# An S4 layer and an int4 SwiGLU on one core: the down weights and the resolvents at another pace, and the second up sum on VectorE

## The reference, cut to what matters

```python
# attn: S4. One kernel K of 1024 taps for all rows, a causal convolution along a row
g = 2.0 / step * ((1.0 - Omega) / (1.0 + Omega))
denom = g[:, None] - Lambda[None, :]                 # 1024 roots x 64 states
cauchy = lambda v: (v[None, :] / denom).sum(-1)      # four of them
at_roots = c * (k00 - k01 * (1.0 / (1.0 + k11)) * k10)
K = ifft(at_roots, L).real
attn = irfft(rfft(u, n=2*L) * rfft(K, n=2*L))[..., :L] + D[0] * u
# ffn: SwiGLU, weights of 4 bits with a scale and a zero for every 64 inputs
Wg, Wu, Wd = dequantize(...)                         # (w - zero) * scale; inter = 2752
h = silu(xn @ Wg.T) * (xn @ Wu.T)
ffn = h @ Wd.T
```

## Time and profile before

| what | us |
|---|---|
| median of three executions | 1499.83 |
| the profiled execution's own time | 1495.27 |
| its span | 1493.5 |
| TensorE busy in the span | 1333.8 (89%) |
| VectorE busy | 957.6 (64%) |
| GpSimd busy | 674.7 (45%) |
| ScalarE busy | 457.3 (31%) |

### The profile page before, as it was taken

The page is one execution under the profiler, slowest core; times in us unless marked ns, Lnnn a source line. Parts: engine busy times, 40 slices in busy tenths (PEclk is TensorE's granted clock), DMA queues, the critical chain, the costliest instruction groups (busy, mean ns, idle before and its releaser), DMA issues. The chain is left out here.

```text
span 1493.5 us, 17048 instructions
## 1 busy us (share of the span) xinstructions
PE 1333.8 (89%) x6299; PEld 630.9 (42%) x6299; DVE 957.6 (64%) x1057; ACT 457.3 (31%) x801; POOL 674.7 (45%) x484
## 2 busy tenths in 40 slices
PE   1557899988998999989999999449999999999998
PEld 1423444433443444434444444124444444444444
DVE  4744478899999898678898988535233332432341
ACT  3533444434444354444444543221000000000000
POOL 3642466766678688687978786341000000000000
PEclk9978999999999999999999999769999999999999
DMA  5301554343433344344444443779756236335431
GB/s 177 86 29 70 225 166 131 125 133 115 132 124 117 131 134 140 124 139 134 142 134 141 139 137 112 233 247 365 248 185 222 92 109 221 92 110 196 126 101 57
DMA packets 164646, 218.09 MB, mean 146 GB/s; under 512 B 41426, under 2 KB 121940, under 8 KB 162644
## 3 DMA queue, kind: packets, MB, share of 16 engines
q1 hardware_dynamic: 163988, 209.86, 42.8%
q10 hardware_dynamic: 576, 7.14, 1.4%
HBM read 139.64 MB, written 77.34 MB: 145 GB/s over the span
## 5 line engine op out<-in xcount | busy, mean ns | idle before, releaser
L1310 PE MATMUL px<-xo,wo 128*128 128x512 f16 x2016 | 473.9, 389 | 59.1 <-ACT py L960 30.2
L1310 PEld LDWEIGHTS px<-xo,wo 128*128 128x128 f16 x2016 | 200.1, 100 | 308.7 <-issue 26.5
L684 POOL TENSOR_TENSOR wo<-wf,wo 128x512 f16<-128x512 f32 x147 | 236.5, 1619 | 71.9 <-ACT wo L918 71.9
L703 POOL TENSOR_TENSOR hs<-hf,hs 128x512 f16<-128x512 f32 x154 | 210.8, 1375 | 103.2 <-ACT hs L953 96.1
L1394 PE MATMUL px<-wd,hr 128*128 128x512 f16 x1056 | 235.0, 382 | 10.7 <-DMA wd<-w_d 10.7
L1310 PE MATMUL pz<-xo,wo 128*128 128x512 f16 x1008 | 233.6, 382 | 0.0
L1394 PEld LDWEIGHTS px<-wd,hr 128*128 128x128 f16 x1056 | 102.6, 98 | 131.1 <-DMA wd<-w_d 11.2
L1310 PEld LDWEIGHTS pz<-xo,wo 128*128 128x128 f16 x1008 | 99.5, 99 | 120.8 <-issue 4.6
L1925 DVE SCALAR_TENSOR_TENSOR acc<-px,acc 128x512 f32<-128x512 f32 x32 | 22.1, 691 | 155.3 <-PE px L1394 151.3
L953 ACT ACTIVATE hs<-hf 128x512 f16<-128x512 f32 x154 | 94.5, 621 | 80.8 <-DVE hf L1569 48.2
L693 POOL TENSOR_TENSOR ds<-wf,ds 128x512 f16<-128x512 f32 x69 | 104.2, 1511 | 33.1 <-ACT ds_more L939 20.1
(11 more groups left out here) (211 smaller groups left out, 1406.5 us busy)
## 6 DMA issues: line engine op xcount, KB each, us to landing
h_d<-hs SPq DMA_DIRECT2D x154, 256.0 KB, 3.7
hr<-h_d SPq DMA_DIRECT2D x56, 704.0 KB, 4.2
w_d<-ds SPq DMA_DIRECT2D x69, 256.0 KB, 3.9
wd<-w_d SPq DMA_DIRECT2D x4, 2816.0 KB, 12.5
sz<-in_sz_gate SPq DMA_DIRECT2D x21, 512.0 KB
sz<-in_sz_up SPq DMA_DIRECT2D x21, 512.0 KB
sz<-in_sz_down SPq DMA_DIRECT2D x20, 512.0 KB
xc_d<-xo SPq DMA_DIRECT2D x8, 1024.0 KB, 10.5
```

What stands on the lines that cost most here:

```text
L684: pool.tensor_tensor(w_dest(t, j, 1), w_place_of(j), w_dest(t, j, 0), ALU.subtract).then_inc(wlo_done, 1)
L703: pool.tensor_tensor(hs[:, j, :, 1, :], h_place_of(p, j), hs[:, j, :, 0, :], ALU.subtract)\
L1310: done = pe.matmul(bank[:, :], wo[t % 2][:, j, wp, k * P:(k + 1) * P], xo[p][:, j, xp, k, :], start=(j in (0, 3) and k == 0 and wp == 0 an ...
```

## The change

- **An even pace for the down weights.** Time is cut in half units: `split_step(n, i)` is 2(n - 3) + i. In step t each engine does its part of split t (`down_step`, on SyncE, GpSimd, ScalarE and VectorE), and words are dequantised in the steps with t mod 7 = 5 and 0. Group 0 starts in unit 2, so seven splits go by in three and a half units, and the last split is that of unit 41's first half. The order of slabs is now a list made to match, and three `ds` buffers serve all.
- **Loads of `wd`.** Each is one load of the whole `wd[j]`. `wd[0]` now lies where the weight words were and is loaded by SyncE after the last split's store; `wd[1]` and `wd[2]` by ScalarE's queue after unit 41, `wd[3]` and `wd[4]` in and after unit 43, `wd[5]` and `wd[6]` by SyncE.
- **The second up sum.** `snap_u3` and GpSimd's `c22` are gone. A `c22` on VectorE adds the bank px to `s5` into `u3`, and product 6 waits for it.
- **VectorE's order.** `c22(n)` stands ahead of `up` and of `c12(n)`.
- **The resolvents** are made at n = 6, 8, ..., 20; their first three scalings go to ScalarE (`scale_angles`, after `snap_s5`). `roots` follow at 22, columns at 24, rows at 26, the scale at 29. The greatest absolute value is found by VectorE and a small matmul in place of GpSimd's reduction.
- `up_nibble` moves behind `snap_u2` on ScalarE.

The core of the diff:

```diff
+def split_step(n, i):
+    return 2 * (n - 3) + i
+def half_steps(t):
+    if t % 7 == 5:
+        return [(t // 7 + 1, 0)] if t // 7 + 1 <= NG else []
+    if t % 7 == 0:
+        return [(t // 7, 1)] if t // 7 <= NG else []
+    return []
...
# products (TensorE)
-                if j in (1, 2, 4, 5, 6):
-                    pe.wait_ge(snap_done, 4 * full(n) + {1: 1, 2: 1, 4: 3, 5: 2, 6: 4}[j])
+                if j in (1, 2, 4, 5):
+                    pe.wait_ge(snap_done, 3 * full(n) + {1: 1, 2: 1, 4: 3, 5: 2}[j])
+                if j == 6:
+                    pe.wait_ge(u2_done, full(n) + 1)
...
# VectorE
+            def down_step(n, i):
+                t = split_step(n, i)
+                for g, h in half_steps(t):
+                    down_words(g, h)
+                if t % 7 == 1 and 0 <= t // 7 <= NG:
+                    d_sum(t // 7, T1)
+                    d_sum(t // 7, T3)
+                if t % 7 == 3 and 0 <= t // 7 <= NG:
+                    d_sum(t // 7, T2)
+                    d_sum(t // 7, T4)
+            def c22(n):
+                dve.wait_ge(prod_done, products_before(n) + TURN_POS[4] + 1)
+                dve.wait_ge(snap_done, 3 * full(n) + 2)
+                if n >= 1:
+                    dve.wait_ge(hf_done, 2 * full_before(n) + 2)
+                dve.tensor_tensor(u3[:, :], px[n % 2][:, :], s5[:, :], ALU.add).then_inc(u2_done, 1)
...
                 gate(2 * g + 1)
-                if g > 1:
-                    d_sum(g - 2, T2)
-                    d_sum(g - 2, T4)
                 h_s12(g - 1, 1)
+                down_step(n, 0)
+                c22(n)
                 up(2 * g + 1)
                 t_sum(2 * g + 1, T1)
                 t_sum(2 * g + 1, T3)
                 s4_work(n)
                 c12(n)
                 h_first(n, 2 * g, 0)
+                down_step(n, 1)
 
                 h_second(n, 2 * g, 0)
                 t_sum(2 * g + 1, T2)
                 t_sum(2 * g + 1, T4)
                 h_s4(g - 1, 1)
-                down_words(g - 1, 0)
+                down_step(n + 1, 0)
                 h_s3(g, 0)
                 s4_work(n + 1)
+                c22(n + 1)
+                down_step(n + 1, 1)
                 c12(n + 1)
                 h_first(n + 1, 2 * g, 1)
 
                 h_second(n + 1, 2 * g, 1)
                 gate(2 * g + 2)
+                down_step(n + 2, 0)
+                c22(n + 2)
                 up(2 * g + 2)
                 t_sum(2 * g + 2, T1)
                 t_sum(2 * g + 2, T3)
...
# SyncE, at the end of phase A
+            sp.wait_ge(wlo_done, 7 * 21 + 3)
+            load_wd(0)
+            for j in (A12, A22, S1, S2, S4):
+                store_h(NG, 0, j)
             sp.wait_ge(prod_done, products_before(42))
             load_hr(0, 0, 0)
             load_hr(0, 0, 1)
```

More of the change, by code:

```diff
@@ L84, with _slabs, down_slab, slab_arrived @@
 PHASE_A = products_before(NU)
+def split_step(n, i):
[6 more added lines that the diff above has]
+    return []
+def _slabs():
+    order = [("gate", 0), ("up", 0), ("gate", 1), ("up", 1)]
+    for n in range(2, 42):
+        if n == 2 or (n >= 4 and n % 2 == 0 and n < 40):
+            order.append(("gate", n // 2 + 1))
+        if n == 40:
+            order.append(("gate", 21))
+        for i in range(2):
+            if i == 1 and n >= 4 and n % 2 == 0 and n < 40:
+                order.append(("up", n // 2 + 1))
+            if i == 0 and n == 3:
+                order.append(("up", 2))
+            for g, h in half_steps(split_step(n, i)):
+                order += [("down", g, h)] if g < NG else [("tail", 0, h), ("tail", 1, h)]
+    return order
+SLABS = _slabs()
+SLAB = {s: m for m, s in enumerate(SLABS)}
+NIBBLES = [sum(s[0] != "tail" for s in SLABS[:m + 1]) for m in range(len(SLABS))]
 def slab_gate(t):
-    return 2 * t if t <= 2 else 6 * ((t - 1) // 2) + (0 if t % 2 else 3)
+    return SLAB["gate", t]
 def slab_up(t):
[L93 to L101, removed]
+    return SLAB["up", t]
+def down_slab(g, kh, half):
+    return SLAB["down", g, half] if g < NG else SLAB["tail", kh, half]
+def slab_arrived(m):
+    return sum(64 if s[:2] == ("tail", 0) else 32 for s in SLABS[m % 2:m + 1:2])
 def split_place(g, j):
-    return 7 * g + D_POS[j] if g < NG - 1 else (70 if g == NG - 1 else 63) + LAST_POS[j]
+    return 7 * g + D_POS[j]
 def sum_place(g, j):
[L111 to L131, removed]
+    return 4 * g + T_POS[j]
+SPLITS = 7 * (NG + 1)
 def conv_pieces(sp_, i):
@@ L704, in h_low @@
                     .then_inc(said, 1)
-            def c22(n):
-                pool.wait_ge(snap_done, 4 * full(n) + 4)
-                pool.tensor_tensor(u3[:, :], u3[:, :], s5[:, :], ALU.add).then_inc(u2_done, 1)
             def h_zero(p):
@@ L733, in _ @@
             x_rstd(5)
-            c22(0)
             w_low(1, B11)
@@ L1789, in _ @@
                 x_low(5, j)
+            c22(0)
             c12(0)
@@ L1807, in _ @@
                 x_low(7, j)
+            c22(1)
             c12(1)
```

522 lines of the change are left out of this document (237 added, 285 removed).

## The result

The changed kernel takes 1539.51 us (median of four runs, 1534.32 to 1541.99) against 1498.51 us for the kernel before beside it (1497.01 to 1501.25): ratio 1.0267, 95% interval 1.0235 to 1.0299. It is 41 us slower; the forecast was 26 us faster. The profiled span (one execution) is 1538.8 us in place of 1493.5.

What follows compares the result with a forecast made beforehand. Phase B was taken as full, with losses in phase A and the transition: 1495.3 + 19 (phase A) - 45 (transition) = 1469.3 us, median 4.6 us above, 1473.8 us. Range 1440 to 1503 us (forecast's own 1460 to 1488).

Steps and rivals of the forecast that it cites:

- clock, put down as one sum: Phase A: 5 us lost to a lower granted clock after idle times of over 3.7 us.
- Transition: Unit 42's end to the flips' end: waits on `wd` and `kshift` go, 3 us left over; 45 us shorter.
- the late load: Rival for the transition: `wd[0]` or first `hr` stays a 10 us wait, more at later pieces; 1494 us, chance 0.09.
- Phase B: The full last stretch, untouched by the change: keeps its length, 463 us from the flips' end.
- Phase A's loss: Time beyond undisturbed units in phase A: 70 us in place of 51.3, so 19 us longer.
- the steady 27 us: Phase A: 3.0 us for each of 9 g, from VectorE's late second up sum and late slabs.
- 2.2 us for each g: Phase A: product 6 waits for VectorE's sum, as the first and third intervals are too long.
- VectorE gains from a freer GpSimd: Phase A: GpSimd loses 1.42 us a unit, worth 0.6 us to VectorE, whose load stays level.
- the first rival: VectorE's intervals shrink as GpSimd starves; phase A no longer or 10 us shorter; 1450 us, chance 0.27.
- Resolvents and roots, 28 us: Phase A: resolvents in VectorE's long intervals, with numerators, roots, columns, rows and scale; 28 us lost (18 to 45).
- Start, 10 us: First units: `up(2)` lands late behind eight stores of x's operands and ScalarE waits; 10 us (0 to 14).
- the slower one: Rival: product 6 waits for VectorE, phase A losing more than 101 us; 1530 us, chance 0.11.

Runs made afterwards that it cites:

- p1: The changed kernel with the second up sum back on ScalarE and GpSimd and the resolvents and roots in their old units; 1520.3 us.
- b1: The kernel before with the second up sum on VectorE and the up nibble after `snap_u2`, pace and resolvents as before; 1557.4 us.
- g1: d1 with cheaper steps chosen for halves of the down weights, and flip and `kshift` loads ahead of unit 41's h stores; 1492.98 us.
- g2: g1 with the second up sum on VectorE again, in the places of the change; 1533.3 us.
- a1: The changed kernel with the second up sum undone: ScalarE's copy of bank x and GpSimd's sum again; 1524.8 us.
- a3: The changed kernel with six of each resolvent's seven VectorE instructions left out; 1513.2 us.
- a4: The changed kernel with the eight stores of x's operands issued later, one in each g; 1529.1 us.
- t1: The changed kernel with the four tail slabs one a step and the first two `hr` loads ahead of five h stores; 1523.4 us.
- f1: d1 with the scales' load of the 20 down slabs left out; 1498.7 us.
- f2: d1 with VectorE's 44 sums of the down weights cut to 32 of 512 columns; 1487.6 us.
- d1: The changed kernel with a1, a4 and t1 together, and each resolvent one unit later, in odd units; 1502.1 us.

## Why the prediction was wrong

Where the losses lie, by units between the marks (us; the forecast's 3.0 us for each g is spread over the units, 4 units to a g):

| units | forecast | before | after | p1 | b1 | g1 | g2 |
|---|---|---|---|---|---|---|---|
| 2 to 5 | 11.5 | 2.5 | 28.0 | 21.5 | 8.6 | 15.4 | 18.8 |
| 6 to 22 (resolvents, roots) | 40.8 | 35.0 | 65.6 | 50.4 | 76.9 | 41.0 | 71.7 |
| 23 to 36 | 10.5 | 11.5 | 23.0 | 16.0 | 28.2 | 18.4 | 35.5 |
| 37 to 39 | 2.2 | 2.2 | 19.6 | 19.9 | 5.9 | 16.6 | 15.5 |
| clock, put down as one sum | 5 | | | | | | |
| all | 70 | 51.1 | 136.2 | 107.7 | 119.6 | 91.5 | 141.5 |

- **Transition**: forecast 45 us, measured 31.8. The waits of the earlier trace rows went as said, and `wd` was in time. What was missed is the late load, with another price: `hr` queued behind five stores, 13.21 us. With it and `kshift` moved, g1 gains 113.7 - 65.3 = 48.4 us, the upper end. Phase B: right.
- **Phase A's loss, put at 70 us and measured at 136.2, is what failed, and in it first the steady 27 us for the second up sum and the slabs.** The working took VectorE's work per interval against 18.13 us and found 69 of 72.5 us, "VectorE still fits on average". It counted no waits on VectorE's own queue. The sum makes VectorE wait for TensorE, 66 to 69 us between 250 and 900 us (after, b1, g2), more than the 3.5 us for each g that were free (27 us for the 31 units there). That `up` and the rest are queued behind `c22` was named; VectorE's idle time ahead of it was priced at nothing. The place was right: in b1 and g2 product 6 waits in units n + 1 and n + 3 (250 to 900 us). The size was not: 2.2 us for each g, where g2 loses 50.0 us more between the marks than g1, 5.3 us for each g (4.9 in units 23 to 36), and b1 68.5 us more than the kernel before, with the nibble moved.
- **The sum is not the whole of it.** Undoing it takes 25.4 of the 136.2 us away (a1). p1, with no sum on VectorE and the resolvents in their old units, still loses 107.7 us, more than the forecast gave to all parts together. Beyond the kernel before it loses 19.0 us in units 2 to 5, 15.4 in 6 to 22, 4.5 in 23 to 36 and 17.7 in 37 to 39. So the pace was priced too low as well, most of all where it begins and ends.
- **VectorE gains from a freer GpSimd**: true, and no gain came of it. A dequantisation's three instructions fell from the lengths of the earlier trace rows to these (620 to 1010 us; count, busy, mean ns, idle), 4.25 us together in place of 4.88:

```profile
L1456 DVE SCALAR_TENSOR_TENSOR wf<-wf,sz 128x1024 f32<-128x1024 f32 x26 | 45.3, 1741 | 0.9
L1455 DVE TENSOR_TENSOR wf<-wf,sz 128x1024 f32<-128x1024 int32 x25 | 41.5, 1659 | 1.9 <-ACT wf L867 1.2
L1453 DVE TENSOR_SCALAR wf<-raw 128x512 int32<-128x512 int32 x25 | 21.3, 851 | 4.8 <-DMA sz<-in_sz_up 4.8
```

  GpSimd is busy for 65% of this stretch, in place of 77%: it has lost the sum, and it waits with the others. This is what the first rival stood on.
- **Resolvents and roots, 28 us**: with 12.8 us of the steady part these units were to lose 40.8 us; the kernel after loses 65.6, against 35.0 before. The resolvents' work alone is worth 26.4 us (a3).
- **Start, 10 us**: the mechanism right (the stores; a wait of 7.39 us at 187.93 on ScalarE), the size off: 22.5 us lost in units 2 and 3, where the kernel before lost 2.5 and the forecast was 10. a4 gives 10.4 back. Against it, the first mark is 8.0 us earlier in the kernel after, 8.5 in g2 against g1, 4.9 in b1 against before: at units 0 and 1 the sum helps, where the prediction had nothing.
- **The end of phase A** was in no term: 19.6 us after the marks of units 37 to 39, where two tail slabs are dequantised in one step and the next gate and up slabs keep ScalarE waiting. Only spreading the tails was tried (t1), and it did not mend it; the cause is open.

```profile
932.70 0.72 ACT L867 ACTIVATE wf<-raw,below 128x512 int32<-128x512 uint8 x1 [6.45 <-DMA sz<-in_sz_gate]
...
955.76 0.72 ACT L867 ACTIVATE wf<-raw,below 128x512 int32<-128x512 uint8 x1 [8.93 <-DMA sz<-in_sz_up]
```

- **The rival nearest to the time** is the slower one, chance 0.11, 1530 us: product 6's wait for VectorE. Its threshold, a loss of over 101 us, was passed (136.2). Its mechanism is not what the kernel after shows: there product 6 waits only 7.1 us for the sum between 250 and 900 us, 18 of the 38 units are over 20.7 us and not all, and VectorE's instructions got shorter and not longer (4.25 us for a dequantisation in place of the rival's 5.5). So its number came out near in part by luck. In b1 and g2 product 6 does wait, 51.1 and 55.6 us, as read above.

What stays open: how the remaining 91.5 us of loss in g1 divide between VectorE's load and slabs (f1 and f2 give the down parts only, 3.4 and 14.5 us); why the sum costs 15 us in one kernel and 40 in another; what the late nibble does in b1; and what the pace costs where it ends.

## What to carry to other kernels

When a step is moved to an engine that is 85 to 97% busy, count what that engine will wait for at the new instruction, not only the work: each wait at the head of an in-order queue is load, and if its producer waits for the same engine, lateness comes back round the loop. Test such a step by adding it to a kernel as well as by undoing it in the kernel after: here undoing gave 15 us, adding 40 (g2) and 58 (b1, with the nibble). And look for what a change costs where it begins and ends, not only in its steady part. At the end of a stage, put the load that the next stage starts with ahead of stores that only have to land some time.

## What was not expected of the hardware

In f2 the down sums are 32 columns wide in place of 512, and three of the four still take half to two thirds of their time. Two of them (d1, then f2; 250 to 900 us, count, busy, mean ns):

```profile
L1552 DVE TENSOR_TENSOR wf<-wf 128x512 f32<-128x512 f32 x9 | 13.8, 1534 | 0.0
...
L1556 DVE TENSOR_TENSOR wf<-wf 128x512 f32<-128x512 f32 x9 | 13.8, 1533 | 0.0
```

```profile
L1552 DVE TENSOR_TENSOR wf<-wf 128x32 f32<-128x32 f32 x9 | 9.3, 1034 | 0.0
...
L1556 DVE TENSOR_TENSOR wf<-wf 128x32 f32<-128x32 f32 x9 | 1.6, 179 | 0.0
```

L1556 follows L1552 at once. The second of the pair takes 179 ns, the first 1034 on average: some 0.85 us of it do not go with its width. The Trainium skill (SBUF — State Buffer, "Who interferes with whom") says that a VectorE instruction with two SBUF inputs and a GpSimd one that reads SBUF exclude each other for the whole instruction; these rows agree with it. Cutting the columns to a sixteenth left most of the first one's time here. What leaving out the instruction would give wasn't run.

Issuing a DMA mostly takes 0.3 to 0.5 us on SyncE's queue, but five stores of 256 KB took 19.81 us to issue behind the three loads of 2816 KB, in a stretch with the DMA engines at 1.02 of their time. In t1, with two `hr` loads ahead of them as well, the same five took this long:

```profile
1008.64 0.91 SPq L558 DMA_DIRECT2D hr<-h_d  x2
1011.73 36.37 SPq L422 DMA_DIRECT2D h_d<-hs  x5
```

The stores also wait for GpSimd's parts of h in this span: 11.2 us in t1, and 10.0 of 37.84 us in g1. That leaves 25 and 28 us that are no such wait. What held the issue isn't shown.
